# A two-layer transformer kernel: the second layer's start, and its dynamic convolution laid out by taps

## The reference

```
# attention part of layer one; b sequences, l = 1024 tokens, H = 16 heads of d = 16, K = 31 taps
avg = cumsum(x, axis=1) / arange(1, l + 1)
ci = avg split into heads                                   # (b*H, l, d)
pc = ci @ W_pe + b_pe                                       # 2*K columns
dyn, gate = pc[..., :K], pc[..., K:]
energy = stt_energy + sigmoid(gate) * dyn                   # per head and tap
w = softmax(energy, axis=-1)                                # over the 31 taps, zero before the first token
out = sum over kk of w[:, :, kk] * padded[:, kk:kk + l, :]  # a causal convolution, a kernel per token
v = layernorm(out @ W_fc.T + residual) * gamma + beta
# ffn part of layer one
h = relu(x @ W1 + b1);  result = h @ W2 + b2
```

## Time and profile before

| | us |
|---|---|
| runs of the kernel before | 3872.47, 3874.77, 3876.25 |
| median | 3874.77 |
| the profiled execution's own time | 3875.27 |
| its span, first to last instruction | 3873.50 |
| retention stage, up to about | 1115 |
| experts, up to the meeting before layer one | 2224.7 |
| layer one | 1649 |

### The profile page before, as it was taken

One profiled execution on the slowest core, in us unless ns is written; L12 is line 12 of the kernel. 1 busy time (PEld: TensorE's weight loads), 2 busy tenths in 40 slices (PEclk: granted clock), 3 DMA queues, 4 the chain that ended last, 5 costly groups with the idle time before them and its releaser, 6 DMA issues.

```text
span 3873.5 us, 70678 instructions
## 1 busy us (share of the span) xinstructions
PE 3402.5 (88%) x27050; PEld 2837.9 (73%) x27050; DVE 2855.6 (74%) x6364; ACT 1948.4 (50%) x3778; POOL 1272.1 (33%) x1014
## 2 busy tenths in 40 slices
PE   4999999999951199999999726999999999999999
PEld 2888888888841188888888715777777777777787
DVE  4677777777757877777777258788888888878864
ACT  2666666666630055555554424555555555555544
POOL 1233333333220045556555433222222222223210
PEclk7999999999975599999999958999999999999999
DMA  4132322222120223333333246555555555555551
GB/s 180 61 102 97 103 99 96 75 80 74 46 65 0 44 73 73 78 85 89 80 72 77 35 106 125 109 116 118 119 118 117 120 122 119 120 118 120 104 102 39
DMA packets 741209, 355.90 MB, mean 92 GB/s; under 512 B 549500, under 2 KB 694248, under 8 KB 740744
## 3 DMA queue, kind: packets, MB, share of 16 engines
q1 hardware_dynamic: 716296, 316.76, 33.3%
q0 software_dynamic: 24576, 34.62, 5.2%
HBM read 215.37 MB, written 135.92 MB: 91 GB/s over the span
## 4 chain that ended last, share of the span: by engine, by line
PE 74%; DVE 14%; issue 4%; ACT 4%; POOL 1%; DMA 1%; SPq 1%; POOLq 0%; another core or an unknown queue 0%; ACTq 0%; DVEq 0%
PE bank L1207 9%; PE bank L1223 8%; PE bank L1795 8%; PE bank L750 8%; PE bank L731 8%; PE bank L1781 8%; PE bank L1753 6%; PE bank L116 5%; PE bank L709 3%; PE bank L1764 2%; DVE hits L1040 2%; PE bank L1735 2%; ACT xh_ L500 2%; PE bank L1190 1%; DVE w L1643 1%
## 5 line engine op out<-in xcount | busy, mean ns | idle before, releaser
L1479 POOL TENSOR_TENSOR energies<-energies,energy 128x496 f32<-128x496 f32 x128 | 173.5, 1356 | 743.1 <-DVE energies L1624 743.1
L988 ACT ACTIVATE bank<-bank,fc_bias 128x512 f32<-128x512 f32 x256 | 169.5, 662 | 407.9 <-PE bank L1207 407.3
L1149 DVE TENSOR_TENSOR hidden_low<-bank,hidden_high 128x512 fp32r<-128x512 f32 x256 | 174.1, 690 | 270.1 <-ACT hidden_high L994 266.6
L1795 PE MATMUL bank<-l_w_high,l_hidden_low 128*128 128x256 f32 x1024 | 310.9, 304 | 52.8 <-DVE l_hidden_low L1687 52.7
L639 DVE TENSOR_TENSOR gT_low<-bank,gT_high 128x512 fp32r<-128x512 f32 x256 | 173.4, 688 | 228.7 <-ACT gT_high L545 228.7
L1128 DVE TENSOR_TENSOR onehot_p<-bank,slot_p 128x1024 bf16<-128x1024 f32 x256 | 311.0, 1215 | 0.0
L750 PE MATMUL bank<-w_high,gT_low 128*128 128x256 f32 x1024 | 308.4, 301 | 0.8 <-DVE gT_low L639 0.8
L539 ACT ACTIVATE bank<-bank,b 128x512 f32<-128x512 f32 x256 | 170.1, 664 | 273.4 <-PE bank L731 270.5
L1687 DVE TENSOR_TENSOR l_hidden_low<-bank,l_hidden_high 128x512 fp32r<-128x512 f32 x256 | 172.9, 686 | 173.7 <-ACT l_hidden_high L1563 173.5
L1795 PE MATMUL bank<-l_w_high,l_hidden_high 128*128 128x256 f32 x1024 | 289.8, 283 | 0.0
L750 PE MATMUL bank<-w_high,gT_high 128*128 128x256 f32 x1024 | 289.2, 282 | 0.0
(11 more groups left out here) (302 smaller groups left out, 11012.7 us busy)
## 6 DMA issues: line engine op xcount, KB each, us to landing
bandT<-bands SPq DMA_DIRECT2D x352, 240.0 KB, 3.6
fc_full<-in_L_ffn_fc_wT SPq DMA_DIRECT2D x32, 1024.0 KB, 4.9
bands<-zeros SPq DMA_DIRECT2D x22, 768.0 KB, 8.6
x<-in_L_attn_x SPq DMA_DIRECT2D x32, 512.0 KB, 6.3
moe_output<-zeros SPq DMA_DIRECT2D x32, 512.0 KB, 7.2
x_after_retention<-x SPq DMA_DIRECT2D x32, 512.0 KB, 3.0
moe_input_and_gates<-xn SPq DMA_DIRECT2D x32, 512.0 KB, 4.1
x<-x_after_retention SPq DMA_DIRECT2D x32, 512.0 KB, 4.1
```

The costliest lines, as they stand in the source:

```text
L1149: v.tensor_tensor(t.hidden.low[:, n % SLICES, :], K.banks[t.bank["expand", i, g, 0]][:, :], t.hidden.high[:, n % SLICES, :], ALU.subtract) ...
L1479: e.tensor_tensor(e1[:, :, :], e1[:, :, :], t.energy[:, :, :], ALU.add).then_inc(s("full_energy"), 1)
L1795: p = pe.matmul(K.banks[6 + ch // 2][:, left:left + D], x, w, start=False, stop=f == KF - 1 and j == 2 and ch % 2 == 1)
```

## The change

Five things are done.

1. SP issues the loads of batch 0 (`row_in`, both halves of `x2` and `moe`) right after the meeting, ahead of all weights. Of the small loads 9 are left in the place of 18 (`w_pe` comes as one block with its zeros from DRAM, `energy` as one row).
2. The biases' preparation goes to a step of its own, `prepare`, at place 17.0 of batch 0, on DVE; at the same place POOL clears the pads, windows and `bandT`. The split of the four quarters goes to steps `take_mlp` at places 25.1, 26.5, 27.9 and 29.3 of batch 0, on ACT and DVE.
3. `w_pe`, `pe_bias`, `energy` and the energies are laid out [tap, head] from the kernel product on. `w` is then written as it is read; the two reductions over taps read with a step of 16 floats. PE's product writes runs of 4 floats with a step of 8.
4. `gated` is two instructions of 248 elements, one for each group of 8 heads.
5. The experts' scatter waits for each pair of blocks by itself.

```diff
@@ expert_pool, "scatter"
-            e.wait_ge(s("gated"), 2 * (i + 1))
...
             for n in range(C):
+                if n % 2 == 0:
+                    e.wait_ge(s("gated"), 2 * i + n // 2 + 1)
@@ order_d
+PREPARE_D = 17.0
+    at(PREPARE_D, "prepare")
+    for n in range(4):
+        at(PREPARE_D + 8.1 + 1.4 * n, "take_mlp", n)
@@ layer_one_tiles
-    t.w_pe = K.tile(ctx, "w_pe", [P, 2, t.HR, KW])
-    t.energy = K.tile(ctx, "energy", [P, H, KW])
+    t.w_pe = K.tile(ctx, "w_pe", [P, 2, KW, t.HR])
+    t.energy = K.tile(ctx, "energy", [P, KW, H])
@@ layer_one_sync
+    for half in range(2):
+        load_half(0, half)
+    e.wait_ge(*K.setup("pool", "bias_rows_zero"))
     for dst, src in loads:
         e.dma_start(dst, src).then_inc(s("d_weights"), 16)
@@ layer_one_pool
+        elif name == "prepare" and b == 0:
+            for i in range(2):
+                e.memset(t.avgT[i][:, :, 0:t.PAD], 0.0)
+                e.memset(t.avgT[i][:, :, t.PAD + K.S:], 0.0).then_inc(s("pool_setup"), 1)
+            e.memset(t.window[0][:, :, :, :], 0.0)
+            e.memset(t.window[1][:, :, :, :], 0.0).then_inc(s("pool_setup"), 1)
+            e.memset(t.bandT[0][:, :, :], 0.0)
+            e.memset(t.bandT[1][:, :, :], 0.0).then_inc(s("pool_setup"), 1)
@@ layer_one_vector
+        elif name == "prepare" and b == 0:
+            prepare()
+        elif name == "take_mlp" and b == 0:
+            (n,) = args
+            parts, _, width = quarters[n]
+            v.wait_ge(*K.setup("scalar", f"l1_mlp_high{n}"))
+            v.tensor_tensor(parts.low, mlp_full(t, n, width), parts.high, ALU.subtract).then_inc(s("vector_setup"), 1)
@@ layer_one_vector, "gated", "energies", "softmax"
-            v.scalar_tensor_tensor(out=e1[:, :, :].rearrange("p (r c) k -> p r (c k)", r=2), in0=t.th[n % 2][:, :, :], scalar=1.0,
-                                   in1=kernel_view(K, t, b, ch, 0), op0=ALU.add, op1=ALU.mult).then_inc(s("gated_energy"), 1)
+            for r in range(2):
+                m = v.scalar_tensor_tensor(out=e1[:, :, r * H // 2:(r + 1) * H // 2], in0=t.th[n % 2][:, r, :].rearrange("p (k c) -> p k c", k=KW), scalar=1.0,
+                                           in1=kernel_view(K, t, b, ch, 0)[:, r, :].rearrange("p (k c) -> p k c", k=KW), op0=ALU.add, op1=ALU.mult)
+            m.then_inc(s("gated_energy"), 1)
...
-            v.tensor_reduce(top[:, :], e1[:, :, :], AX_X, ALU.max).then_inc(step, c.up())
+            v.tensor_reduce(top[:, :], e1[:, :, :].rearrange("p k h -> p h k"), AX_X, ALU.max).then_inc(step, c.up())
...
-            v.tensor_reduce(total[:, :], t.e[n % 2][:, :, :], AX_X, ALU.add).then_inc(step, c.up())
+            v.tensor_reduce(total[:, :], t.e[n % 2][:, :, :].rearrange("p k h -> p h k"), AX_X, ALU.add).then_inc(step, c.up())
...
-            v.tensor_tensor(t.w[n % 2][:, :, :].rearrange("p k h -> p h k"), t.e[n % 2][:, :, :],
-                            total[:, :].unsqueeze(2).to_broadcast([P, H, KW]), ALU.mult).then_inc(s("w"), 1)
+            v.tensor_tensor(t.w[n % 2][:, :, :], t.e[n % 2][:, :, :], total[:, :].unsqueeze(1).to_broadcast([P, KW, H]), ALU.mult).then_inc(s("w"), 1)
@@ layer_one_tensor, "kernel_product"
-                    out = pair[r][:, 0:4 * t.RW].rearrange("p (a j c) -> p j a c", a=2, j=KD)[:, j, :, :]
+                    out = pair[r][:, 0:4 * t.RW].rearrange("p (k j q) -> p j k q", j=KD, q=t.HR)[:, j, :, :]
```

More of the change, by code:

```diff
@@ L1483, in layer_one_scalar @@
     s, D, KD, C, HC, KF, TT, NT, H = K.sem, K.D, K.KD, t.C, t.HC, t.KF, K.TT, K.NT, K.HEADS
-    for n, (parts, _, width) in enumerate(mlp_quarters(K, t)):
-        full = t.x2[n + 3][:, :, :].rearrange("p c d -> p (c d)").rearrange("p (k n) -> p k n", n=width)
-        e.wait_ge(s(f"l1_mlp{n}"), 16)
-        e.copy(parts.high, full).then_inc(s("scalar_setup"), 1)
-    e.wait_ge(s("d_weights"), t.loads)
-    e.wait_ge(*K.setup("pool", "windows"))
+    quarters = mlp_quarters(K, t)
     for name, b, *args in ordered(K.B, t.steps):
@@ L1584, in layer_one_vector @@
-    v.tensor_scalar(t.ones[:, :], K.ident[:, :], 0.0, 1.0, ALU.mult, ALU.add)
-    v.tensor_scalar(t.w_pe[:, 0, :, :], t.w_pe[:, 0, :, :], 0.5, None, ALU.mult)
-    v.tensor_scalar(t.pe_full[:, 0, :, :, :], t.pe_full[:, 0, :, :, :], 0.5, None, ALU.mult).then_inc(step, c.up())
-    v.wait_ge(step, c.n)
-    for bias, full in ((t.pe_bias[:, :, :, :, :].rearrange("o a j q k -> o (a j q k)"), t.pe_full[:, :, :, :, :].rearrange("o a j q k -> o (a j q k)")),
-                       (t.out_bias[:, :, :].rearrange("o a d -> o (a d)"), t.out_full[:, :, :].rearrange("o a d -> o (a d)"))):
-        v.tensor_copy(bias, full).then_inc(step, c.up())
-        v.wait_ge(step, c.n)
-        v.tensor_scalar(full, full, t.pick[:, 0:1], None, ALU.mult).then_inc(step, c.up())
+    quarters = mlp_quarters(K, t)
@@ new lines, in prepare @@
+    def prepare():
+        v.wait_ge(s("d_weights"), t.loads)
+        v.wait_ge(*K.setup("pool", "exponents"))
+        v.tensor_scalar(t.ones[:, :], K.ident[:, :], 0.0, 1.0, ALU.mult, ALU.add)
+        v.tensor_scalar(t.w_pe[:, 0, :, :], t.w_pe[:, 0, :, :], 0.5, None, ALU.mult)
+        v.tensor_scalar(t.pe_full[:, 0, :], t.pe_full[:, 0, :], 0.5, None, ALU.mult).then_inc(step, c.up())
+        v.wait_ge(step, c.n)
+        for bias, full in ((t.pe_bias[:, :, :, :].rearrange("p a k c -> p (a k c)"), t.pe_full.rearrange("p a c -> p (a c)")),
+                           (t.out_bias[:, :, :].rearrange("o a d -> o (a d)"), t.out_full[:, :, :].rearrange("o a d -> o (a d)"))):
+            v.tensor_copy(bias, full).then_inc(step, c.up())
+            v.wait_ge(step, c.n)
+            v.tensor_scalar(full, full, t.pick[:, 0:1], None, ALU.mult).then_inc(step, c.up())
+            v.wait_ge(step, c.n)
+            v.scalar_tensor_tensor(out=bias, in0=bias, scalar=t.pick[:, 1:2], in1=full, op0=ALU.mult, op1=ALU.add).then_inc(step, c.up())
@@ L1594, in layer_one_vector @@
         v.wait_ge(step, c.n)
-        v.scalar_tensor_tensor(out=bias, in0=bias, scalar=t.pick[:, 1:2], in1=full, op0=ALU.mult, op1=ALU.add).then_inc(step, c.up())
-    v.wait_ge(step, c.n)
-    v.memset(t.top[0][:, :], 0.0).then_inc(s("vector_setup"), 1)
-    v.wait_ge(*K.setup("vector", "rows_split"))
+        v.memset(t.top[0][:, :], 0.0).then_inc(s("vector_setup"), 1)
     for name, b, *args in ordered(K.B, t.steps):
@@ L1729, in layer_one_tensor @@
                 rows = slice(r * P // 2, (r + 1) * P // 2)
-                pe.matmul(pair[r][:, 0:4 * t.RW], t.ones[rows, :], t.pe_bias[rows, :, :, :, :].rearrange("o a j q k -> o (a j q k)"), start=True, stop=False)
+                pe.matmul(pair[r][:, 0:4 * t.RW], t.ones[rows, :], t.pe_bias[rows, :, :, :].rearrange("p a k c -> p (a k c)"), start=True, stop=False)
             for j in range(KD):
```

117 lines of the change are left out of this document (61 added, 56 removed).

## The result

| | before | after |
|---|---|---|
| median of 5 runs, us | 3874.24 | 3895.16 |
| lowest and highest | 3872.11, 3876.25 | 3892.65, 3897.23 |
| span of the profiled execution | 3873.50 | 3893.40 |

The ratio is 1.0054, its 95% interval 1.0043 to 1.0066: 20.9 us slower, where 3 faster was forecast. The time lies in the range, but on the other side of "no change".

What follows compares the result with a forecast made beforehand. PE sets the pace, DVE limits in one 22 us stretch per batch, and the filling is a chain of hand-overs. -19.1 + 1.4 + 5.4 + 2.8 + 6.9 - 0.8 = -3.4, forecast 3872 us, range 3858 to 3902.

Steps and rivals of the forecast that it cites:

- Part 7: Experts' scatter: POOL starts once ACT finishes the first pair, so the meeting comes 0.8 us earlier; other halves 0.
- Part 1: Loads first: the first `moe` lands after 5.06 us, so DVE starts 19.1 us earlier (14.9 if landing takes 9.3).
- Part 2: `prepare`: biases ahead of the scan are free on DVE; POOL's later `row_bias` addition holds the scan, +1.4 us.
- Part 3: Layout by taps: +0.46 us of DVE per chunk, bounds -0.28 and +0.53; +1.8 us in batch 0.
- Part 5: Batch 1 and up to full pace: seven more chunks on a busy DVE, two of which meet POOL, +2.8 us.
- Part 4: Quarters: in four chunks of batch 0 a DVE subtraction delays POOL's addition by 0.9 us each, +3.6 us.
- Part 6: Full pace: only DVE work after its last wait for PE counts; 0.55 us per batch, 12.5 batches, +6.9 us.
- no play at all at full pace: Rival: DVE's short waits are hand-overs that shift; six chunks reach PE's wait, 2.8 us per batch, 3900 us; chance 0.15.
- free stepped reading: Rival: reductions reading with a 64-byte step cost nothing extra, so a chunk is -0.28 us: 3853 us; chance 0.08.
- Its own signs: Trace marks of a right forecast, among them PE's `l_hidden_low` wait 4.4 to 4.7 us per batch, a batch 96.2 long.
- PE's product slows: Rival: PE's stepped writes into its bank cost +0.47 us per chunk, +52 us in all: 3924 us; chance 0.10.

Runs made afterwards that it cites:

- kernel 3: The kernel before plus one extra DVE largest-value over half of the heads in chunks 0 to 4, from batch 2 on: 3887.6 us, ratio 1.0030.
- kernel 6: kernel 3 with ACT's exponential of chunk 3 moved behind its copy of window 8: 3875.9 us, ratio 1.0005.
- kernel 2: The kernel before with the layout by taps alone (and nine small loads in the old place): 3904.8 us, ratio 1.0072.
- kernel 4: The kernel before plus one extra DVE largest-value over half of the heads in chunks 5 to 7, from batch 2 on: 3891.4 us, ratio 1.0045.
- kernel 5: The changed kernel with ACT's exponential of chunk 3 moved behind its copy of window 8: 3890.1 us, ratio 1.0045.
- kernel 1: The changed kernel with the old layout by heads put back: 3862.4 us, ratio 0.9969.
- kernel 7: kernel 1 with DVE's quarter splits behind the subtraction of the largest value and POOL's clears behind its first `row_bias` addition: 3861.1 us, ratio 0.9969.
- kernel 9: kernel 1 with quarter splits moved, and the second half's statistics, then chunk 7's largest value, put behind the last two `hidden_low`: 3830.3 us, ratio 0.9887.

## Why the prediction was wrong, point by point

| part | predicted | measured |
|---|---|---|
| 7, meeting | -0.8 | +1.3, scatter |
| 1 and 2, to the average | -17.7 | -15.4 |
| 3 and 5, layout while filling | +4.6 | +6.1 |
| 4, quarters | +3.6 | +4.3 |
| 6, full pace | +6.9 | +23.5 |
| sum | -3.4 | +19.9 |

**Part 6 is the step that failed**, with 16.6 of the 23.3 us. It has three pieces per batch. (a) The wait at the old place grew by 0.78 (43.1 to 51.7 in the 11 batches), for 0.55. The mechanism was right, and so nearly was the size: in one batch DVE takes 21.54 from its last wait for PE to the last `hidden_low` before and 22.05 after (2961.09 to 2983.14), +0.51; the held `w` swallowed what came ahead of it (1.88 for 3.00). (b) "The chunks before 2955 add 2 us, which DVE's waits for ACT and PE take up": wrong. They reach PE by ACT's queue, 0.45 per batch. DVE's own wait for PE of 1.26 showed play at that one place; it said nothing on who waits for DVE's results in between. Kernels 3 and 6 differ by that queue alone, and by 11.7 us. (c) 0.49 per batch is slower work of PE. The prediction put this at nothing without a reason. Windows of the changed kernel, PE alone, two batches one after the other (busy, granted clock, DMA share, GB/s):

```profile
2510.88:2607.30 96.42, 91.44 (x827) 0.98 0.57 117
2607.30:2705.10 97.80, 92.66 (x827) 0.97 0.55 115
```

The same 827 instructions take 1.2 us more in the second. The granted clock is at 0.50, the lower of its two levels, once in each batch, at the wait for `l_hidden_low` or just behind it (a product of the contraction takes 0.41 for 0.28). In the first of these two batches it is there for 3.4 us, from 2594.4, all of them busy; in the second for 6.8, from 2690.1. Over the 11 batches one stretch before lasts 6.8 and ten last 3.4; after it is five and six. The busy time lost at the lower level, read in windows of 0.25 us, is 19.6 us before and 23.9 after: 4.3 of the 5.4. The long kind goes with the longer wait: where PE waits some 4.7 for `l_hidden_low` it comes 5, 6, 3 and 6 times in 11 (changed, kernels 2, 4, 5), where it waits 3.9 to 4.0 it comes 1, 0, 2, 1 and 2 times (before, kernels 1, 3, 6, 7). What decides in a single batch was not settled.

**The rival "no play at all at full pace"** (3900) comes nearest in its time, and its argument for itself, that short waits are hand-overs that shift, is what happened at ACT. Its price of 2.8 per batch was too high, since the 1.26 of play is real: 0.55 of it is used up in the changed kernel, and kernel 6 hides 2.2 us of DVE work in it and in DVE's waits for ACT.

**Part 3** per chunk: +0.34 and +0.34 for the reductions, -0.35 for `w`, +0.07 for the gating in two (0.74 from first start to last end, as the timeline has it, for 0.67), in all +0.40 for the +0.46 reckoned. The rival of free stepped reading is false: 1.005 for 0.664, a step of 64 bytes costs 0.69 ns an element where 32 bytes cost 0.75 in the earlier trace rows. The Trainium skill's rule on lines of 16 bytes ("SBUF — State Buffer", "Specifications (TRN2)") holds here in both directions.

**Parts 3 and 5 while filling** came to 6.1 for 4.6: kernel 1 shows this as the difference of two traces. From batch 0's average to batch 1's it takes 74.73 by taps and 72.03 by heads (+2.7, for 1.8), from there to batch 2's 80.33 and 76.91 (+3.4, for 2.8). So too much was counted as swallowed where POOL holds DVE, it seems; in which chunks was not followed up. (The prediction's own 2.3 less three times 0.2 is 1.7, not 1.8.)

**Part 1** fell short by 1.7: the first `moe` took 7.05 us to land (2226.77 to 2233.82), between the 5.06 and the 9.3 of the two bounds, of which 5.06 was taken; SP issued it 0.4 earlier than reckoned. **Part 2** was right: the scan, held by POOL's addition, took 3.93, +1.64 for +1.4, and the biases were free; kernel 7 confirms the cause with 2.27. **Part 4**: three additions of POOL took 2.14, as reckoned; in chunk 3 the addition took its 1.23, but the subtraction took 1.67 and ended 1.1 after it.

**Its own signs** were met in part: the wait of 4.7 per batch, the reductions at 1.005 and `w` at 0.676 are as it had them for a right forecast. A batch of 97.2 us for 96.2, the first addition on DVE 10.25 us after the first clear for 8.5 to 9, and a cast of 1.22 among the biases for at most 0.8 are not. The new wait is of PE for ACT; its list had only waits for DVE.

**Part 7** can't be told: the first clear comes at 2223.7 to 2225.9 in the five profiled kernels with the old wait and at 2223.1 to 2226.0 in the nine with the new one, with means of 2224.9 and 2224.6.

**"PE's product slows"** (3924) is false: 369 ns for 368, though each product writes runs of four floats with a step of eight. The Trainium skill's sentence that any access that is not contiguous slows matmuls significantly ("PSUM — Partial Sum Buffer", "Specifications (TRN2)") is not borne out for this pattern.

## What to carry to other kernels

Time added to an engine that is not the bound is not absorbed because that engine later waits for the bound. List instead, for each of its results in the stretch, what stands behind the waiting instruction on the third engine's queue: one exponential ahead of one copy made 2.2 us per batch cost 13 us, and behind it nothing measurable. A wait of the bound engine is also the place to look for gains: the order of three DVE steps ahead of it was worth some 30 us (kernel 1 to kernel 9, the quarters' place included), as much as the layout costs. Count such a wait at more than its length: the changed kernel, with a longer wait, has 0.49 us per batch more of PE's busy time for the same work, and kernel 9, with a shorter one, 0.99 less than kernel 1. And a stepped read costs what a stepped write does here (0.34 and 0.35 us for 496 elements), so a layout that trades one stepped write for two stepped reads loses.

## What the runs showed of the hardware

- A DVE instruction of 512 elements that started 0.35 us into an addition of POOL ended only behind all that POOL had back to back: 6.36 us for 0.49, across nine POOL instructions (kernel 7, one case). In the changed kernel the cast of 512, started 0.08 ahead of the same clears, took 1.22. The Trainium skill, "SBUF — State Buffer", "🔬 SBUF: two separate sides", says that DVE and GpSimd share a pair of ports, that DVE takes it in its two-port modes or with two inputs from SBUF, and that the one that starts first holds it for its whole instruction while the other fully blocks. The trace agrees with the blocking, but here it lasted for nine instructions and not one.
- With a stall of 4 to 5 us in a batch the granted clock goes to its lower level (0.50) for 3.4 us and in some batches for 6.8, and the two kinds differ by up to 1.2 us of busy time with the same work. With the stall of 2.4 us of kernel 9 it stays at the upper level in 5 of 11 batches.
- Products that write PSUM in runs of 16 bytes with gaps of 16 are as fast as those that write runs of 124 floats (369 ns and 368).
